# Weights of two experts from a tanh in the expert stage instead of an exponential in the graph stage

## The reference

```python
logits = tokens @ router_w.T                # 3125 x 8
probs = softmax(logits)
rw, re = top_k(probs, 2)                    # two best experts of each token
rw = rw / max(rw.sum(-1), 1e-12)
...
h = gelu(tokens @ w1[e] + b1[e])            # exact gelu, 256 -> 256
y = h @ w2[e] + b2[e]
out = out + combine[:, e] * y               # combine holds rw at the chosen experts, else 0
```

## Time and profile before

| | us |
|---|---|
| median of 3 runs | 1010.29 |
| lowest, highest run | 1008.53, 1013.03 |
| span of the profiled execution | 1013.6 |
| busy in it: PE, DVE, ACT, POOL | 859.1, 644.0, 416.8, 699.5 |

### The profile page before, as it was taken

The page is one execution under the profiler, slowest core; times in us unless marked ns, Lnnn a source line. Parts: engine busy times, 40 slices in busy tenths (PEclk is TensorE's granted clock), DMA queues, the critical chain, the costliest instruction groups (busy, mean ns, idle before and its releaser), DMA issues.

```text
span 1013.6 us, 19598 instructions
## 1 busy us (share of the span) xinstructions
PE 859.1 (85%) x6332; PEld 528.8 (52%) x6332; DVE 644.0 (64%) x2171; ACT 416.8 (41%) x1087; POOL 699.5 (69%) x503
## 2 busy tenths in 40 slices
PE   3878878988999999999999999999399961999930
PEld 2433433435445444545545555555398851899920
DVE  3699998896576365365455665656667764555534
ACT  3544543332454334334334443443144441666620
POOL 4788888888887878888778888887403568544420
PEclk7699998996999999999999999999699975999975
DMA  9865664545465555455546565435944424344459
GB/s 292 172 112 85 97 119 57 83 60 104 70 132 90 81 89 81 73 103 81 91 52 104 79 129 76 49 35 77 295 130 116 126 85 136 109 132 126 128 135 271
DMA packets 144169, 113.10 MB, mean 112 GB/s; under 512 B 106847, under 2 KB 129955, under 8 KB 143942
## 3 DMA queue, kind: packets, MB, share of 16 engines
q1 hardware_dynamic: 79988, 71.74, 25.3%
q0 software_dynamic: 56928, 25.42, 24.0%
q10 hardware_dynamic: 7154, 14.68, 4.6%
HBM read 72.00 MB, written 40.89 MB: 111 GB/s over the span
## 4 chain that ended last, share of the span: by engine, by line
PE 37%; POOL 10%; DMA 7%; DVE 5%; issue 4%; ACT 1%; ACTq 0%; SPq 0%; POOLq 0%; DVEq 0%
POOL edge_sums L694 9%; PE ps L1321 5%; PE ps L1532 5%; PE ps L1543 5%; PE ps L1461 3%; PE ps L1128 3%; DMA edge_sums<-sums,addr 3%; DMA r2t<-expert_outputs 2%; PE ps L1271 2%; PE ps L1257 2%; PE ps L1308 2%; PE ps L1517 1%; PE ps L1451 1%; PE ps L1297 1%; POOL routed_rows L713 1%
## 5 line engine op out<-in xcount | busy, mean ns | idle before, releaser
L694 POOL DMA_INDIRECT edge_sums<-sums,addr x360 | 565.7, 1571 | 136.7 <-issue 105.0
L1684 DVE TENSOR_SCALAR oh<-node,dsrc 128x500 bf16<-128x500 int16 (+1 forms) x392 | 116.7, 359 | 73.3 <-PE ps L1321 73.0
L921 ACT ACTIVATE r<-ps 128x500 f32<-128x500 f32 (+1 forms) x224 | 103.4, 549 | 72.0 <-PE ps L1257 71.9
L1321 PE MATMUL ps<-oh,r2t 128*64 128x500 bf16 (+1 forms) x1176 | 130.7, 359 | 1.4 <-DVE oh L1684 1.4
L1128 PE MATMUL ps<-edges,same 128*128 128x65 f32 x720 | 101.2, 286 | 12.1 <-ACT sums L754 4.6
L1647 DVE TENSOR_TENSOR r2t<-ps,r 125x4096 f32<-125x4096 f32 x25 | 110.3, 4413 | 0.0
L1128 PEld LDWEIGHTS ps<-edges,same 128*128 128x128 f32 x720 | 91.8, 200 | 35.5 <-issue 28.2
L1587 DVE SCALAR_TENSOR_TENSOR same<-srow,src_f,below 128x128 f32<-128x128 int32 x360 | 103.6, 345 | 3.6 <-DMA srow<-in_src_row 2.7
L1321 PEld LDWEIGHTS ps<-oh,r2t 128*64 128x64 bf16 x1176 | 59.1, 110 | 71.2 <-issue 39.2
L725 POOL DMA_INDIRECT expert_outputs<-r x56 | 54.4, 972 | 56.0 <-DVE r L2043 51.2
L1175 PE MATMUL ps<-r2t,r 125*32 125x512 f32 x400 | 60.1, 727 | 34.2 <-DVE r2t L1647 34.2
(11 more groups left out here) (284 smaller groups left out, 1381.7 us busy)
## 6 DMA issues: line engine op xcount, KB each, us to landing
srow<-in_src_row SPq DMA_DIRECT2D x45, 512.0 KB
edges<-in_edge_attr SPq DMA_DIRECT2D x22, 512.0 KB
r<-routed_rows SPq DMA_DIRECT2D x56, 129.0 KB, 2.1
r<-hpre_rows SPq DMA_DIRECT2D x12, 500.0 KB, 4.2
edge_sums<-sums,addr POOLq DMA_INDIRECT x360
r2t<-in_ew SPq DMA_DIRECT2D x4, 1024.0 KB, 9.3
hpre_rows<-r ACTq DMA_DIRECT2D x16, 250.0 KB, 2.5
edge_sums<-r SPq DMA_DIRECT2D x4, 884.0 KB, 13.9
```

Source lines behind the costliest of these rows:

```text
L694: pool.indirect_dma_start(out=tables[k], out_offset=bass.IndirectOffsetOnAxis(ap=addr[:, j:j + 1], axis=0), in_=sums[:, j % OR, :], in_off ...
L921: act.activation(phT[:, R % 2, h, 0:n], bank(BP[h], 128, 0, n), ACT.Square).then_inc(pair_squares, 1)
L1321: m = mm(ps[EA * a:EA * (a + 1), BD * BANK:BD * BANK + n], lhsT=parts3[:, (DCH - 1 - 2 * w // DW) * DW + (2 * w + a) % DW, s, :], rhs=oh[: ...
L1684: v.tensor_scalar(oh[:, (2 * i + a) % OHS, 0:nt * P].rearrange("p (t n) -> p t n", t=nt), node16[:, 0:nt, :], dsrc[:, 2 * w + a:2 * w + a ...
```

## The change

The tables' function Exp leaves the graph stage: `exps` goes, and `runner` stays a score difference. `follow` signals `sh_ready` no more. `weights` has four instructions in place of six: it writes minus the difference beside the first choice and the difference beside the second, and waits for nothing of ACT. In the expert stage ACT gets `choice_tanh`, which makes tanh of half of the column for step s+2, after the Gelu of step s+1; for steps 0 and 1 it stands behind the first Gelu. `output_rows` on DVE waits for it and writes 0.5 + 0.5 times it in place of the copy. After its last tile ACT loads the table of Gelu.

```diff
--- before.py
+++ after.py
@@ -265,6 +265,7 @@
         ys = carve([128, SB, C])
         y_idx = carve([128, SB], u32)
         y_w = carve([128, SB])
+        y_t = carve([128, SB])
         FT = 5
         b2_rows = srow[:, :, :].rearrange("p h c -> p (h c)").bitcast(fp32)[:, 0:E * C]
 
@@ -395,7 +396,7 @@
         lg_ps = sem("lg_ps")
         lg_ready = sem("lg_ready")
         sh_ready = sem("sh_ready")
-        ex_ready = sem("ex_ready")
+        tanh_ready = sem("tanh_ready")
 
         mask_ready = sem("mask_ready")
         ranks_ps = sem("ranks_ps")
@@ -1046,12 +1047,8 @@
                 sd(t - 1, 1 - u)
                 tok_copy(t - 3, 1 - u)
 
-            def exps(b):
-                t0, t1 = BATCHES[b]
-                act.wait_ge(sh_ready, 2 * b + 2)
-                act.activation(runner[:, t0:t1], runner[:, t0:t1], ACT.Exp).then_inc(ex_ready, 1)
-            tiles(gnn, 4, [(t1 + 6, lambda b=b: exps(b)) for b, (t0, t1) in enumerate(BATCHES[:-1])])
-            exps(len(BATCHES) - 1)
+            tiles(gnn, 4)
+            act.preload_act_table(ACT.Gelu)
 
             act.wait_ge(table_ready, 1)
             for e in range(1, E, 2):
@@ -1066,6 +1063,14 @@
                 wait(act, xs_ps, s + 1)
                 wait(act, eh_ps, s - 1)
                 act.activation(xsT[:, h % 2, :], bank(h % 2, 128, 0, C), ACT.Copy).then_inc(xsT_ready, 1)
+
+            def choice_tanh(st):
+                if not some(st):
+                    return
+                s, h, nth = st
+                act.wait_ge(xs_loaded[h], nth * 16 + 16)
+                wait(act, idx_ready, s - SB + 1)
+                act.activation(y_t[:, h:h + 1], xs[:, h, C:C + 1], ACT.Tanh, scale=0.5).then_inc(tanh_ready, 1)
 
             def gelu(st):
                 if not some(st):
@@ -1090,10 +1095,13 @@
                     xsT_copy(step_at(st, 2))
                     weigh(step_at(st, -2))
                     gelu(step_at(st, 1))
+                    choice_tanh(step_at(st, 2))
             xsT_copy((0, 0, 0))
             xsT_copy((1, 1, 0))
             act.wait_ge(table_ready, 2)
             gelu((0, 0, 0))
+            choice_tanh((0, 0, 0))
+            choice_tanh((1, 1, 0))
             steps(act, expert_steps, SB, 2)
 
             for h in range(SB):
@@ -1935,10 +1943,8 @@
                 r_, z_, w_, k_ = red[:, 0:n_], shifted[:, 0:n_, :], rest[:, 0:n_, :], pick[:, 0:n_, :]
                 one, two = chosen[:, 0, t0:t1, :], chosen[:, 1, t0:t1, :]
                 link(v.scalar_tensor_tensor(w_, one, -1e30, z_, ALU.mult, ALU.add))
-                v.tensor_reduce(runner[:, t0:t1], w_, AX.X, ALU.max).then_inc(sh_ready, 1)
-                v.wait_ge(sh_ready, 2 * b + 1)
+                link(v.tensor_reduce(runner[:, t0:t1], w_, AX.X, ALU.max))
                 link(v.tensor_tensor(w_, w_, wide(runner[:, t0:t1]), ALU.subtract))
-                v.sem_inc(sh_ready)
                 first_of(w_, k_, r_, two, n_)
                 link(v.tensor_tensor(both[:, 0:E * n_].rearrange("p (e t) -> p e t", e=E), one.rearrange("p t e -> p e t"), two.rearrange("p t e -> p e t"), ALU.add))
                 v.tensor_tensor_scan(upto[:, 0:E * n_], keeps[n_], both[:, 0:E * n_], 0.0, ALU.mult, ALU.add).then_inc(mask_ready, 1)
@@ -1946,16 +1952,12 @@
             def weights(b):
 
                 t0, t1 = BATCHES[b]
-                r_ = red[:, 0:t1 - t0]
-                v.wait_ge(ex_ready, b + 1)
-                link(v.tensor_scalar(r_, runner[:, t0:t1], 1.0, 1e-12, ALU.add, ALU.max))
                 if b >= len(second_rows):
                     v.wait_ge(routed_rows[1 + b % len(second_rows)], 16 * (BATCHES[b - len(second_rows)][1] - BATCHES[b - len(second_rows)][0]))
                 twin = second_rows[b % len(second_rows)][0:P, 0:t1 - t0, :]
-                link(v.reciprocal(r_, r_))
-                v.tensor_copy(xl_all[0:P, t0:t1, C], r_)
+                v.tensor_scalar(xl_all[0:P, t0:t1, C], runner[:, t0:t1], -1.0, None, ALU.mult)
                 v.tensor_copy(xl_all[0:P, t0:t1, C + 1], dst_row[:, t0:t1])
-                v.tensor_tensor(twin[:, :, C], runner[:, t0:t1], r_, ALU.mult)
+                v.tensor_copy(twin[:, :, C], runner[:, t0:t1])
                 v.tensor_scalar(twin[:, :, C + 1], dst_row[:, t0:t1], float(N), None, ALU.add)
 
             def place(b):
@@ -2039,7 +2041,8 @@
                 s, h, nth = st
                 wait(v, xs_loaded[h], nth * 16 + 16)
                 wait(v, ys_stored[h], nth * 16)
-                v.tensor_copy(y_w[:, h:h + 1], xs[:, h, C:C + 1])
+                v.wait_ge(tanh_ready, s + 1)
+                v.tensor_scalar(y_w[:, h:h + 1], y_t[:, h:h + 1], 0.5, 0.5, ALU.mult, ALU.add)
                 v.tensor_copy(y_idx[:, h:h + 1], xs[:, h, C + 1:XF]).then_inc(idx_ready, 1)
 
             def add_b2(st, col):
```

## The result

The changed kernel takes 1005.24 us (median of 6 runs, 1002.63 to 1009.32) against 1013.28 us of the kernel before (median of 6 runs in all, 1008.53 to 1015.49). The ratio is 0.9924 with a 95% interval of 0.9899 to 0.9948: some 7.7 us less, 5.3 to 10.2. The forecast was 6.4 us less.

The account below looks back on a forecast made before the run. TensorE was taken to set the pace, and the end of place(2) ahead of GpSimd's queue to start the expert stage. Savings of 1.44 + 2.95 + 1.75 + 0.3 = 6.4 us off 1010.3 gave 1003.9 us, range 1000.0 to 1008.0.

Parts of the forecast that it names:

- The issue of batch 2: GpSimd's queue: batch 2's rows, begun at 817.88 before, due 6.4 us earlier at 811.5, with GpSimd free near 809.7.
- The sum of 6.4 us: Graph stage, ahead of place(2): savings of 1.44 + 2.95 + 1.75 + 0.3 us, moving all 26 GpSimd issues by 6.4 us.
- 1.44, 2.95, 1.75 and 0.3 for both: Savings in us: TensorE at batches 0 and 1, VectorE's sum at batch 2, follow's dropped semaphore at batches 0 and 1.
- The time of 1003.9 us: Whole kernel: the earlier median of 1010.3 us less 6.4 us of savings.
- With no idle microsecond I take both losses as gone: Batch 1 on TensorE: the idle time and the slow clock (0.60) behind it both vanish, 2.95 us saved.
- the clock stays low: Rival, chance 0.20: batch 1's clock fell for another reason; batch 1 gives 1.44 us, whole saving 4.9, time 1005.4.
- Four instructions instead of six: Weights on VectorE: fewer instructions, the first without a wait, bring it to the next sum sooner; no separate size.
- The slower rival: Expert stage, chance 0.06: tables change every step for Tanh and Gelu, 4.3 us a step, 129 us more, 1133 in all.

Follow-up runs that it names:

- exp_last_two: Changed kernel with Exp and its wait put back for batches 3 and 4 alone; stretch (batch 0's lead to expert stage) 87.89 us, ratio to kernel before 0.9920.
- place_early: Changed kernel with place of batches 0 to 2 one body earlier; lead-to-expert-stage stretch 86.10 us against 87.98, ratio to the kernel before 0.9931.
- exp_first_three: Changed kernel with Exp and the weights' wait for it put back for batches 0 to 2; lead-to-expert-stage stretch 92.10 us, ratio to the kernel before 0.9978.
- exp_three_chain: Changed kernel with Exp, wait and two linked old weights instructions put back for batches 0 to 2; lead-to-expert-stage stretch 92.99 us, ratio to kernel before 0.9993.

## Why the prediction was right

*Where the gain is made.* The prediction put it at `place(2)` and GpSimd's queue behind it. exp_last_two shows that what lies later costs nothing, and place_early that an earlier `place` pulls the expert stage along. The issue of batch 2, forecast at 811.5, began at 810.75 in an execution whose stretch began 0.79 us earlier.

*The sum of 6.4 us.* It came out to a tenth (6.40), because it was taken from intervals of the one trace that it is compared with. Its terms have their sizes, too: from before to after the two tiles lose 1.43 us at batch 0 and 2.94 at batch 1, VectorE comes to batch 2's sum 1.71 us sooner, and the tiles of the two `follow` lose 0.12 and 0.16, where the prediction had 1.44, 2.95, 1.75 and 0.3 for both. What did not hold is that all of it hangs on the Exp and the wait for it, as I expected of exp_first_three. The runs divide it, each figure from a difference of two single traces, good to some 0.3 us: 88.50 - 87.98 = 0.5 us for the second signal and the wait as such, 92.10 - 88.50 = 3.6 us for the tables, 92.99 - 92.10 = 0.9 us for the two linked instructions behind the wait, and 94.38 - 92.99 = 1.4 us for the clock.

*The time of 1003.9 us.* That 1005.24 came within 1.3 us of it is in part luck. The six runs of before have a median 3.0 us above the 1010.3 that I started from, and the two medians lie 8.0 us apart instead of 6.4; the two misses cancel in part.

*The step that was too sure* is "With no idle microsecond I take both losses as gone", priced at 2.95 us for batch 1. Gone they are, but the 1.5 us of clock in them belong to the one execution of before that was profiled. In exp_three_chain the same stops left the clock full, and the kernel before would then have lost some 5.0 us where I counted 6.4. That the rival "the clock stays low" did not come about is shown: the clock is 1.00 in the changed kernel.

*Four instructions instead of six.* I wrote that VectorE comes to the sum sooner and gave it no price. Behind a wait that TensorE feels, two linked instructions lengthen each stop from 0.57 to 1.00 us, and VectorE's timeline in exp_three_chain shows how:

```profile
770.33 0.17 DVE L1970 TENSOR_SCALAR r<-r 125x6 f32<-125x6 f32 x1 [1.88 <-ACT r L1056]
770.53 0.19 DVE L1973 RECIPROCAL r<-r 125x6 f32<-125x6 f32 x1
770.76 0.17 DVE L1974 TENSOR_SCALAR r<-r 125x6 f32<-125x6 f32 x1
770.84 0.17 DVE L1975 COPY r<-dst_row 125x6 f32<-125x6 f32 x1
```

What follows a linked instruction (the first two) begins 0.20 and 0.23 us after it, what follows an unlinked one 0.08: together the 0.43 us by which the stop grows. Without the wait I would expect them to lie in VectorE's idle time; that wasn't tried.

*The expert stage.* The Tanh measured 0.20 us against 0.21 assumed, and is hidden. The slower rival had the right mechanism and too high a price: 115.6 us for Sigmoid where I had added up 129. The sum laid the operations end to end, 4.3 us a step; in the trace the copy begins 0.09 us before Sigmoid's end and the weighing 0.11 before the copy's, and the step is 4.12. Its condition failed: of Exp, Sigmoid and Tanh, only Tanh stands beside Gelu in these runs. By the list in the Trainium skill, "ScalarE: Activation LUTs" (Table sets: the hidden batching unit), Tanh would have needed a load against Gelu; the trace of the changed kernel shows a single table load from 715 us on, the early one, and 56 Tanh between 112 Gelus without any.

*The rest of the measured gain.* 7.7 us were measured, 5.3 to 10.2. The trace explains 6.4, and no run settles whether the difference is more than the spread.

## What to carry to other kernels

Before a function leaves one stage for another, look at which table the new stage keeps loaded: the same weights cost nothing as a tanh beside Gelu and 115.6 us as a sigmoid. A wait for a neighbour is cheap as long as it fits into the idle time of the waiting engine; here the table loads inside it made 3.6 of the 6.4 us. Linked instructions behind such a wait lengthen it by all of their own time, here by 0.43 us. Find the queue behind which the next stage starts, and count only the delays ahead of its last wait.

## What the runs showed of the hardware that was not expected

The granted clock after a stop isn't settled by the stop: behind seven stops of TensorE of 0.99 or 1.00 us at the same places of the program it fell three times. Over the two tiles that could be measured in full it was 0.66 both times, a mixture of 2.4 and 1.2 GHz, and each cost its tile 1.5 us (5.05 and 5.04 us to the next L1461 or L1477, against 3.54 with a full clock); the third shows as an L1461 of 3.17 us. A table load is 1.28 us, and where a function was waiting it began 0.01 to 0.02 us behind the load, in every trace. And in the changed kernel VectorE's copy of 128x512 took 2.72 and 2.81 us at the start of the expert stage, while GpSimd added the residual, against 0.41 us in the next one and 0.62 or 0.63 in most after that. The long copies went with GpSimd's adding in the traces of before (2.50 and 2.81 us) and after alike; no run parts the two, so the cause is not shown.
